# Last mixture of experts: all eight experts' weights on chip, chosen by registers in PE's matmuls

## What is computed

```python
h = rmsnorm(hidden, attn_norm_w)
... grouped attention: 16 query heads, 4 key heads of 128, with rotation and a causal mask ...
hidden = hidden + attn @ o_w.T
tok = rmsnorm(hidden, ffn_norm_w).reshape(T, D)          # T = 1024 tokens, D = 256
probs = softmax(tok @ gate_w.T)                          # 8 experts
topv, topi = top_k(probs, 2); topw = topv / sum(topv)
eg = einsum('td,eid->eti', tok, wg)                      # i: 176 hidden channels
eu = einsum('td,eid->eti', tok, wu)
eo = einsum('eti,edi->etd', silu(eg) * eu, wd)
moe_out = einsum('te,etd->td', combine, eo)              # combine holds topw at the chosen two
```

## Time and profile before

| | us |
|---|---|
| time, median of 3 runs | 1291.06 (1290.24 to 1292.5) |
| time of the profiled execution | 1285.59 |
| its span, first to last instruction | 1283.8 |
| PE busy | 1088.0 (85%) |
| DVE busy | 704.6 (55%) |
| ACT busy | 506.5 (39%) |
| POOL busy | 320.5 (25%) |

### The profile page before, as it was taken

The page is one execution under the profiler, slowest core; times in us unless marked ns, Lnnn a source line. Parts: engine busy times, 40 slices in busy tenths (PEclk is TensorE's granted clock), DMA queues, the critical chain, the costliest instruction groups (busy, mean ns, idle before and its releaser), DMA issues.

```text
span 1283.8 us, 20548 instructions
## 1 busy us (share of the span) xinstructions
PE 1088.0 (85%) x7122; PEld 824.0 (64%) x7138; DVE 704.6 (55%) x1700; ACT 506.5 (39%) x1787; POOL 320.5 (25%) x440
## 2 busy tenths in 40 slices
PE   1788886899997788799999999996888999985684
PEld 0355443899996466588888888884555556553463
DVE  5877745212223788854555445555656666664334
ACT  0255562232321466643334333333445555542121
POOL 5544210222322355420000000002122222210562
PEclk9999997899998699999999999998989999998797
DMA  6443305898883070000000000140000000000785
GB/s 191 120 134 108 99 15 178 308 333 317 326 328 114 1 263 2 1 28 20 1 2 1 1 1 1 33 132 1 1 1 9 5 5 5 6 5 9 238 254 183
DMA packets 59731, 121.31 MB, mean 94 GB/s; under 512 B 9049, under 2 KB 37481, under 8 KB 53713
## 3 DMA queue, kind: packets, MB, share of 16 engines
q1 hardware_dynamic: 52169, 106.61, 24.8%
q0 software_dynamic: 4416, 12.06, 2.9%
q10 hardware_dynamic: 3044, 1.33, 0.4%
HBM read 107.29 MB, written 12.49 MB: 93 GB/s over the span
## 4 chain that ended last, share of the span: by engine, by line
PE 62%; DVE 17%; issue 7%; ACT 6%; DMA 4%; POOL 2%; SPq 1%; ACTq 0%; DVEq 0%; POOLq 0%
PE P L819 6%; PE P L829 6%; PE P L1742 4%; PE P L1735 4%; PE P L1787 4%; PE P L1751 4%; ACT big L2139 3%; DVE small L440 2%; PE P L2659 2%; PE P L1880 2%; PE P L1760 2%; PE P L1775 2%; PE P L1886 2%; PE P L288 2%; PE P L316 2%
## 5 line engine op out<-in xcount | busy, mean ns | idle before, releaser
L139 POOL TENSOR_TENSOR lrs<-lve,mhalf 128x1 f32<-128x1 f32 x64 | 36.7, 574 | 363.5 <-DVE lve L130 332.0
L440 DVE TENSOR_REDUCE small<-P 128x2 f32<-128x512 f32 x128 | 83.4, 682 | 38.6 <-PE P L288 37.9
L2050 ACT ACTIVATE big<-P,small 128x128 f32<-128x128 f32 x128 | 45.4, 367 | 145.0 <-DVE small L2228 145.0
L859 ACT ACTIVATE big<-P,big 128x128 f32<-128x128 f32 x184 | 52.6, 369 | 123.2 <-PE P L819 101.6
L510 ACT ACTIVATE big<-P 128x512 f32<-128x512 f32 x128 | 72.4, 598 | 60.4 <-PE P L301 55.3
L819 PE MATMUL P<-big 128*128 128x128 f32 x736 | 88.0, 279 | 0.4 <-DMA big<-b_w 0.2
L819 PEld LDWEIGHTS P<-big 128*128 128x128 f32 x736 | 85.8, 195 | 1.2 <-issue 0.6
L829 PE MATMUL P<-big 128*128 128x256 f32 x368 | 83.1, 379 | 0.0
L288 PE MATMUL P<-big 90*128 90x256 bf16 x256 | 55.6, 307 | 31.8 <-DMA big<-scr_qk 17.2
L2219 DVE COPY big<-P 128x512 f32<-128x512 f32 x32 | 22.1, 692 | 107.0 <-PE P L1751 107.0
L952 DVE COPY big<-P 128x256 f32<-128x256 f32 x23 | 9.8, 425 | 125.4 <-PE P L829 125.4
(11 more groups left out here) (380 smaller groups left out, 2578.5 us busy)
## 6 DMA issues: line engine op xcount, KB each, us to landing
big<-b_w SPq DMA_DIRECT2D x23, 1028.0 KB
big<-b_w SPq DMA_DIRECT2D x23, 1024.0 KB
big<-scr_qk SPq DMA_DIRECT2D x96, 96.0 KB
big<-i_wgu SPq DMA_DIRECT2D x23, 352.0 KB
big<-moe_y SPq DMA_DIRECT2D x16, 256.0 KB, 4.1
big<-i_wd SPq DMA_DIRECT2D x23, 176.0 KB
scr_qk<-big SPq DMA_DIRECT2D x8, 384.0 KB
moe_x<-XN SPq DMA_DIRECT2D x16, 128.0 KB, 1.7
```

The source lines that it names most:

```text
L440: dve.tensor_reduce(negM[:, h, :], P[:, h % 2, :].rearrange("p (c s) -> p c s", c=2), AX.X, ALU.max, negate=True).then_inc(a_max, 1)
```

## The change

All eight experts' weights get a place of their own in `big1`: `i_w1` in columns 10752 to 16384 and `i_w2` in columns 0 to 4096 of the first 88 partitions. SP loads them with four large DMAs during the grouped attention, each behind a wait for the space: the gate and up weights, 2 x 1408 KB, when the attention before is over (`e_x` at 8); the down weights, 2 x 704 KB, when the last row's keys and values are formed (`h_pkv` at 16) and when the 30th of the 32 query groups is (`h_pq` at 30). These waits stand ahead of the gate's load and of all eight row stores in SP's stream. SP's loop over the 23 blocks goes away, with its register loads.

PE now loads the 23 entries of `eb` into 23 registers, with the same bounds, after its wait for the 8th step of the routing and before its wait for the 13th. `up(j)` and `down(j)` address the weights through the register of block j; `up(0)` waits once for all weights. The last loads' destination moves to another part of `big1`.

```diff
+        i_w1 = big1[:, 10752:16384].rearrange("p (e k n) -> p e k n", e=NE, k=KD)
+        i_w2 = big1[0:IC, 0:4096].rearrange("p (e c d) -> p e c d", e=NE, c=2)
+        i_G2 = big1[:, 6144:10240].rearrange("p (b w d) -> p b w d", b=B, w=2)
-        i_w1 = [ir1.view([128, KD, 2 * I3]) for _ in range(NW)]
-        i_w2 = [ir1.view([IC, 2, D]) for _ in range(NW)]
...
         def s8_sp(sp):
+            sp.wait_ge(e_x, B)
+            for e in (0, 4):
+                sp.dma_start(i_w1[:, e:e + 4].rearrange("p e k n -> p e (k n)"),
+                             i_wgu[e:e + 4].rearrange("e p n -> p e n")).then_inc(i_wu, 16)
+            sp.wait_ge(h_pkv, 2 * B)
+            sp.dma_start(i_w2[:, 0:4].rearrange("p e c d -> p e (c d)"),
+                         i_wd[0:4].rearrange("e p n -> p e n")).then_inc(i_wd2, 16)
+            sp.wait_ge(h_pq, NM - 2)
+            sp.dma_start(i_w2[:, 4:8].rearrange("p e c d -> p e (c d)"),
+                         i_wd[4:8].rearrange("e p n -> p e n")).then_inc(i_wd2, 16)
             sp.dma_start(i_gs, i_gate.rearrange("(k p) e -> p k e", p=128)).then_inc(i_ld, 16)
             for b in range(B):
                 sp.wait_ge(xn_ready, 8 * B + b + 1)
                 sp.dma_start(XD[128 * b:128 * b + 128, :], XN[:, b, :]).then_inc(i_xd, 16)
...
-            sp.wait_ge(cst_p, 6)
-            sp.wait_ge(i_pos, IPOS0 + 8)
-            for j in range(NB):
-                e = sp.value_load(eb[0:1, j:j + 1], min_val=0, max_val=NE - 1)
-                if j == 3:
-                    sp.wait_ge(i_xs[1], IXS0[1] + 16)
-                if j >= NW:
-                    sp.wait_ge(i_up, j - NW + 1)
-                weights1(j, e)
-                if j >= NW:
-                    sp.wait_ge(i_dn, j - NW + 1)
-                weights2(j, e)
...
             pe.wait_ge(cst_p, 6)
+            pe.wait_ge(i_pos, IPOS0 + 8)
+            _, experts = nc.values_load_multi_w_load_instructions(eb[0:1, 0:NB], engines=[mybir.EngineType.PE], min_val=0,
+                                                                  max_val=NE - 1)
             pe.wait_ge(i_pos, IPOS0 + 13)
             slots_pe(pe, i_rank)
...
             def up(j):
-                pe.wait_ge(i_w[j % NW], IW0[j % NW] + 32 * (j // NW) + 32)
+                if j == 0:
+                    pe.wait_ge(i_wu, 32)
+                    pe.wait_ge(i_wd2, 32)
...
-                    m = pe.matmul(P[:, j % 2, 0:2 * I3], xgT[j % 2][:, k, :], i_w1[j % NW][:, k, :], start=(k == 0),
+                    m = pe.matmul(P[:, j % 2, 0:2 * I3], xgT[j % 2][:, k, :],
+                                  i_w1[:, bass.ds(experts[j], 1), k, :].rearrange("p a n -> p (a n)"), start=(k == 0),
                                   stop=(k == KD - 1))
...
-                    m = pe.matmul(P[:, 6 + j % 2, 0:D], i_hT[j % 2][:, c, :], i_w2[j % NW][:, c, :], start=(c == 0),
+                    m = pe.matmul(P[:, 6 + j % 2, 0:D], i_hT[j % 2][:, c, :],
+                                  i_w2[:, bass.ds(experts[j], 1), c, :].rearrange("p a d -> p (a d)"), start=(c == 0),
                                   stop=(c == 1))
```

More of the change, by code:

```diff
@@ L2567, in s47_pool @@
             out_rms(B - 1)
-        NW = 6
+        i_w1 = big1[:, 10752:16384].rearrange("p (e k n) -> p e k n", e=NE, k=KD)
+        i_w2 = big1[0:IC, 0:4096].rearrange("p (e c d) -> p e c d", e=NE, c=2)
+        i_G2 = big1[:, 6144:10240].rearrange("p (b w d) -> p b w d", b=B, w=2)
         ir1 = Arena(big1)
         ir1.at = 4096
-        i_w1 = [ir1.view([128, KD, 2 * I3]) for _ in range(NW)]
-        i_w2 = [ir1.view([IC, 2, D]) for _ in range(NW)]
         i_si, i_hs = ([ir1.view([128, I3]) for _ in range(2)] for _ in range(2))
@@ L2581, in build @@
         i_gs = sm.view([128, KD, NE])
-        i_w = [sem("i_w0"), sem("i_w1"), i_z] + b_w
-        IW0 = [0] * 3 + [32 * len(range(u, NB, 3)) for u in range(3)]
+        i_wu, i_wd2 = sem("i_wu"), sem("i_wd2")
         i_xs = b_xg + [a_stk[2][0], a_stk[2][1], e_max, e_bias, e_rz, e_pn]
@@ L2611, in s8_sp @@
             sp.dma_start(steps, rows(b_steps)).then_inc(m_ld, 16)
-            sp.wait_ge(cst_p, 6)
-            sp.wait_ge(i_pos, IPOS0 + 8)
-            for j in range(NB):
-                e = sp.value_load(eb[0:1, j:j + 1], min_val=0, max_val=NE - 1)
-                if j == 3:
-                    sp.wait_ge(i_xs[1], IXS0[1] + 16)
-                if j >= NW:
-                    sp.wait_ge(i_up, j - NW + 1)
-                weights1(j, e)
-                if j >= NW:
-                    sp.wait_ge(i_dn, j - NW + 1)
-                weights2(j, e)
             sp.wait_ge(b_sc, 32 * NB)
             for b in range(B):
-                sp.dma_start(G2[:, b], YD[0:2 * NT, :].rearrange("(w b p) d -> b p w d", w=2, p=128)[b]).then_inc(
+                sp.dma_start(i_G2[:, b], YD[0:2 * NT, :].rearrange("(w b p) d -> b p w d", w=2, p=128)[b]).then_inc(
                     b_ga[b // 2][0], 16)
@@ L2763, in s8_dve @@
                         dve.wait_ge(i_add, IADD0 + 2 * b + 1)
-                    dve.scalar_tensor_tensor(out=X[:, b, :], in0=G2[:, b, w, :], scalar=share[:, b:b + 1],
+                    dve.scalar_tensor_tensor(out=X[:, b, :], in0=i_G2[:, b, w, :], scalar=share[:, b:b + 1],
                                              in1=X[:, b, :], op0=ALU.mult, op1=ALU.add).then_inc(i_add, 1)
```

## The result

| | before | after |
|---|---|---|
| median of 5 runs each, us | 1290.24 (1286.26 to 1292.5) | 1297.63 (1291.0 to 1301.14) |
| profiled execution, us (span) | 1285.59 (1283.8) | 1301.14 (1299.5) |
| TensorE clock granted, mean | 0.955 | 0.942 |
| L907, the routing's long step, starts at | 1187.61 | 1195.91 |
| from there to the last instruction | 96.2 | 103.6 |

The ratio after to before is 1.006, 95% interval 1.0035 to 1.0086: the change makes the kernel slower, by about 7.4 us. The forecast was +3.2 (1294.3, range 1285 to 1301). Which chip the first measurement had isn't known.

A forecast was written before the change was run, and what follows sets the result against it. Bound: the serial routing-to-first-gather chain, then PE through 23 blocks. Table +7.4, addresses +0.5, gather -0.3, loop -4.4 gave +3.2: 1288.8 us profiled, plus 5.5 for the runs' median, 1294.3; range 1285 to 1301.

The forecast's parts named there:

- The table read: Before PE's slots: loading 23 entries (6.1 us) and checking them (5.8) delays slots and first gather, +7.4 us on the path.
- rival 1: Stage 8's loop: all delays go (-8.7), 1290.0, chance 0.2; second half, table also in one fetch (+1.6), 1284.2, chance 0.12.
- Addresses in the loop: PE's address instructions, 0.13 us each, 0.5 per block, hidden behind a wait except in first and last block: +0.5 us.
- rival 3: Loop: matmuls with a register address hold PE, exposing 0.5 us per block, say +8, 1302; chance 0.08.
- The gather's flight: First gather before the loop: its flight shortens without weight loads beside it, from 2.73 us toward 2.42, -0.3 us.
- moved loads: Four weight DMAs, 4.2 MB, moved to the attention, where DMA is idle: cost zero, or half a us each if exposed.
- SP's queue: Waits ahead of the gate's load and row stores: last opens at the 30th query group; cost zero, 35 us to spare.
- The loop: Stage 8's 23 blocks: weight loads leave, returning part of 8.7 us lost to late signals; the middle taken, -4.4 us.
- Rival 2: Loop: late signals belong to the profiled execution, so timed runs regain at most 0.5 us; sum +7.1, 1298.2; chance 0.15.
- Rival 4: Start of the loop: weights arrive late for the first block's up; no chance worth a number.
- what would show it: Trace signs: read from 1185.7 to 1197.6 with slots then, blocks 2.49 us apart, PE's wait before up 0.3 to 0.5 shorter.

The follow-up runs named there:

- cheap read: Changed kernel with the table two words further on and the 23 bounds checks left out: ratio 0.997 (0.9954 to 0.9986) to the kernel before, chip A.
- the two kernels on A without the read's cost: Changed kernel with constant experts, no read or register addresses (0.9983, -2.2 us), and the cheap read (0.997, -3.9 us), each against the kernel before.
- gathers first: Changed kernel with cheap read, a buffer per block, all 23 gathers ahead of the first scatter: ratio to before 0.9979 on chip B, 1.0071 on C.
- plain gathers: Changed kernel with its 23 gathers replaced by SP's plain loads of 128 consecutive rows, full-cost read kept: ratio 0.9949 to the kernel before, chip A.
- the last run: The cheap read's kernel with scatters from the 4th, 7th and 10th waiting for one more result, so POOL rests: ratio 0.9979 to before, chip D.

## Why the prediction was right, and where it was not

The side and the range were right; the likeliest time was 3.3 us too low. Of its two large terms the table's was right, and the loop's rested on a misreading.

- **The table read, +7.4.** Right, and for the reasons given. Load 5.6 against 6.1 forecast, checks 6.5 against 5.8, two errors that partly cancel; from the start of the load (1194.0) to the slots (1206.28) 12.3 against 11.9; slots 7.9 later relative to L907, L916 7.7, first gather 7.7, first transposes 7.2. A load entry by entry fits, at 5622 / 23 = 244 ns. That it may also go at 2282 / 23 = 99 ns, with the table two words further on and the checks left out, lay inside my bounds, but I had no such case. The Trainium skill, "Runtime: NRT & Kernel Launch", section "Instruction fetch mechanics", has about 200 ns per register, even in bulk; the two loads measured here, from SBUF, lie above and below it. The second half of rival 1 asked for slots before 1196 to turn the sum round. The cheap read has them (2.3 us behind L907's start) and does turn it, to 0.997, but by 3.9 us and not by 6.9: rival 1's other condition, a loop without delays, isn't met there (7.8 lost).
- **Addresses in the loop, +0.5.** Nothing to be seen. The instructions are there, 0.056 us each at the median; in a quiet block the two of `up` start 0.14 apart, so my 0.13 with gap was about right:

```profile
L2653 PEldq FUSED_REGOPS  x46: 46/56/65, 1213.2 to 1276.3; - x46
```

  Quiet blocks are 2.49 us apart with and without them, so matmuls with a register address held nothing here, and rival 3 falls.
- **The gather's flight, -0.3; moved loads, 0; SP's queue, 0.** From POOL's first gather to the first transposes it is 2.92 us in place of 3.43, so -0.5; the other two hold. In SP's queue I had the wrong wait open last: it is the one for the last row's keys and values (L1868 ends at 1146.95, the load behind it starts at 1146.98), not the one for the 30th query group. The eight stores begin at 1148.27, still ahead of their last row.
- **The loop, -4.4. This is the step that failed.** "The delays stop when the weights stop" was a misreading. So was "0.19 at most" for SP's register work in the first mixture: its loads took up to 0.477 there, its comparisons up to 0.187. Three rows of the kernel before, which I hadn't set side by side, would have told: two of POOL, one of the stretch behind them.

```profile
1246.24 0.97 POOL L2771 DMA_INDIRECT big<-moe_x,big  x1 [0.30 <-issue]
1249.10 0.99 POOL L2786 DMA_INDIRECT moe_y<-big  x1 [1.89 <-DVE big L2743]
```

```profile
1255.00:1260.00 5.00, 5.00 (x26) 3.71 (x25) 2.21 (x7) 1.20 (x4) 1.96 (x3) 1.00 0.61 201
```

  1246.24 is the last gather. The last long period between two blocks' transposes runs from 1247.64 to 1251.60, and from there on they are 2.49 apart, with weights still coming at 201 GB/s: the delays stopped with the gathers, ahead of the weights. And POOL's timeline in that loop shows six transfers without a pause, then some 2 us in which it waits for DVE, three times over. I had said that the quiet rows have scatters but no gathers, and then took a middle value instead of asking which of the two streams the stalls follow. What came back is -0.5 us in one pair of profiles and +1.0 in the other. The number fared better than the reading: without its table term the forecast is -4.2, and the timed runs of the two kernels on A without the read's cost are -2.2 (-4.5 to +0.1) and -3.9 (-5.9 to -1.8). That is luck, as the stalls which the term was to remove are still there in both; what the gain is made of isn't shown, and 4.4 was the middle of two ends.
- **Rival 2, the late signals belong to the profiled execution.** Its sum (+7.1) is the nearest to what was measured first (+7.4; on C +5.4), but its reason doesn't hold. The gathers first on chip C took 1301.28 us in the profiled execution with its standstill, and 1299.43, 1301.23 and 1301.68 in the others; and plain gathers gain 12 us or more in timed runs where the profile shows the stalls gone. The Trainium skill's rule, "NOTIFIC — the notification-queue block", section 7.1, that the block holds its producers back inside rather than lose a record, isn't needed for this; nor would it tell why the same program stalls on C and not on B, profiled on both. It isn't excluded either as a part of the cause: the other executions too have a span and a clock on record, so how little was recorded in them isn't known. What stays open is the last run, where the profile is over 6 us shorter from L907 on than the profiles of before (89.7 against 95.9 and 96.2), and the timed runs gain at most 5.7.
- **Rival 1, first half** (all delays go, 1290.0) fell with the loop. **Rival 4** never came near: `up(0)` waits for no weights.

Two further points of "what would show it": slots at 1206.28 less the 8.3 of the execution are 1198.0, against 1197.6 named. And PE's median wait ahead of `up` is gone from its own instruction (51 ns now, 894 before): it stands ahead of the address instruction behind it now, which waits for DVE, with 0.6 us left at the median.

## What to carry to other kernels

A step that an engine's sequencer has to do one entry at a time belongs where that engine waits anyway, and its length depends on details (here the table's place and the checks of its entries) that are cheaper to change than the design around it. When a stall ends together with a stream, list everything else that ends there too, and look at each engine's pauses before naming the cause. When a loop keeps its length, split it into idle and busy time and look at the clock before saying that nothing changed. On the chips that stalled, POOL's indirect transfers did best with pauses between them: count its time per block against the block's, and don't pile them up at the front on the strength of one chip.

## What the runs showed of the hardware

- While POOL issues indirect transfers back to back, other engines see PE's signals late on some chips (waits of up to 16.6 us on C; of 4.3 to 6.7 on A and 5.3 on the unknown one; on D, where only the kernel with rests was profiled, they are late but stop PE little), and not at all on another (B, 36 in a row). The kernel before takes 1282.0 us on B and 1289.5 to 1291.4 on A, C and D. POOL busy with clears of 0.97 us, scatters between them, did nothing on B, where nothing would have; whether it does on the others wasn't tried, nor were gathers alone with pauses. What holds the signals isn't known.
- One load of 23 registers on PE took 5.62 to 5.63 us with the table at word 9906 of its buffer, a multiple of 8 bytes, in the four kernels that have it there, and 2.28 with it at 9908, a multiple of 16, in the four that have it there. These four also leave out the bounds checks; neither edit was made alone.
- Each bounds check of a register costs PE's sequencer 0.28 us: 0.146 of comparison, 0.018 of assertion and the gaps.
- With weights at 249 to 256 GB/s beside the loop it loses 8.9, 9.1 and 10.9 us on chips that stall, without them 7.4 to 9.4; PE is idle 7.0, 5.5 and 7.4 us of that, and 4.3 to 6.1. At 299 GB/s, a DMA share of 0.97, PE's weight loads waited up to 0.8 us for the plain gathers of the same queue.
